# Expert gate and up products: the 96-column chunks share a phase with 128-column ones

## The reference

```
g = jnp.einsum('ech,emh->ecm', buf, Wg)
u = jnp.einsum('ech,emh->ecm', buf, Wu)
out = jnp.einsum('ecm,ehm->ech', jax.nn.silu(g) * u, Wd)
```

## Time and profile before

| | |
|---|---|
| median of 3 runs | 1557.19 us |
| the 3 runs | 1549.15, 1557.19, 1557.39 us |
| span of the profiled execution | 1550.6 us |
| instructions | 30285 |
| TensorE busy | 1471.4 us, 95% of the span |
| VectorE, ScalarE, GpSimd busy | 1132.1, 959.0, 724.0 us |

### The profile page before, as it was taken

The page is one execution under the profiler, slowest core; times in us unless marked ns, Lnnn a source line. Parts: engine busy times, 40 slices in busy tenths (PEclk is TensorE's granted clock), DMA queues, the critical chain, the costliest instruction groups (busy, mean ns, idle before and its releaser), DMA issues.

```text
span 1550.6 us, 30285 instructions
## 1 busy us (share of the span) xinstructions
PE 1471.4 (95%) x10344; PEld 1217.4 (79%) x10344; DVE 1132.1 (73%) x2021; ACT 959.0 (62%) x1897; POOL 724.0 (47%) x894
## 2 busy tenths in 40 slices
PE   6999998999999979599999999999999999999898
PEld 4788887778888767488888888888888888776675
DVE  6677666745888788777777787777777787757666
ACT  4566566644566566677777777777777777731111
POOL 2122225242232155356565655556565655447573
PEclk9999999999999999899999999999999999999999
DMA  6012112332221231398787778777787778567574
GB/s 211 1 63 82 51 60 70 103 93 75 63 76 42 71 108 38 122 370 298 265 296 265 262 259 286 271 268 262 265 297 265 261 261 285 183 213 246 149 216 156
DMA packets 116629, 280.25 MB, mean 181 GB/s; under 512 B 17984, under 2 KB 23104, under 8 KB 116544
## 3 DMA queue, kind: packets, MB, share of 16 engines
q1 hardware_dynamic: 98800, 228.25, 43.4%
q0 software_dynamic: 15360, 50.34, 10.1%
q10 hardware_dynamic: 2384, 0.53, 0.2%
HBM read 235.69 MB, written 43.38 MB: 180 GB/s over the span
## 4 chain that ended last, share of the span: by engine, by line
PE 48%; DVE 3%; issue 2%; POOL 2%; DMA 1%; another core or an unknown queue 1%; ACT 0%; DVEq 0%; SPq 0%; POOLq 0%
PE e_gu L2608 19%; PE e_gu L2610 9%; PE e_dn_rest L2636 6%; PE e_tr L49 3%; PE e_dn_main L41 3%; PE e_dn_main L43 3%; PE e_dn_main L42 3%; DVE h_acc L2901 2%; POOL h_yk L2818 1%; DMA h_yk<-y_dram,h_idx 1%; DVE h_h_raw L2932 0%; DMA e_raw_u<-in_L_ffn_Wu_dram 0%; DVE h_hid L2917 0%; PE h_gt L41 0%
## 5 line engine op out<-in xcount | busy, mean ns | idle before, releaser
L2371 POOL TENSOR_TENSOR e_hid<-e_h_raw,e_hid 128x128 fp32r<-128x128 f32 (+1 forms) x192 | 165.6, 863 | 223.4 <-ACT e_hid L2436 223.4
L2608 PE MATMUL e_gu<-e_xT_hi_lo,e_wg 128*128 128x384 f32 (+1 forms) x768 | 231.9, 358 | 0.6 <-issue 0.6
L2608 PE MATMUL e_gu<-e_xT_hi_lo,e_wu 128*128 128x384 f32 (+1 forms) x768 | 230.6, 356 | 0.0
L2610 PE MATMUL e_gu<-e_xT_hi_lo,e_wu 128*128 128x192 f32 (+1 forms) x768 | 193.4, 252 | 0.0
L2610 PE MATMUL e_gu<-e_xT_hi_lo,e_wg 128*128 128x192 f32 (+1 forms) x768 | 193.2, 252 | 0.0
L2379 POOL TENSOR_TENSOR e_wd<-e_raw_d,e_wd 96x512 fp32r<-96x512 f32 x64 | 131.4, 2053 | 36.1 <-ACT e_wd L2421 36.1
L2431 ACT ACTIVATE e_low<-e_gu 128x384 f32<-128x384 f32 (+1 forms) x192 | 93.2, 486 | 83.5 <-PE e_gu L2610 56.2
L2514 DVE TENSOR_TENSOR e_total<-e_gu,e_low 128x384 f32<-128x384 f32 (+1 forms) x192 | 105.6, 550 | 53.3 <-issue 44.5
L2608 PEld LDWEIGHTS e_gu<-e_xT_hi_lo,e_wg 128*128 128x128 f32 (+1 forms) x768 | 138.3, 180 | 5.8 <-issue 1.6
L2610 PEld LDWEIGHTS e_gu<-e_xT_hi_lo,e_wg 128*128 128x128 f32 (+1 forms) x768 | 140.1, 182 | 1.4
L2608 PEld LDWEIGHTS e_gu<-e_xT_hi_lo,e_wu 128*128 128x128 f32 (+1 forms) x768 | 137.9, 180 | 3.8
(11 more groups left out here) (426 smaller groups left out, 3953.7 us busy)
## 6 DMA issues: line engine op xcount, KB each, us to landing
e_raw_g<-in_L_ffn_Wg_dram SPq DMA_DIRECT2D x64, 704.0 KB
e_raw_u<-in_L_ffn_Wu_dram SPq DMA_DIRECT2D x64, 704.0 KB
e_raw_d<-in_L_ffn_Wd_dram SPq DMA_DIRECT2D x64, 512.0 KB, 6.2
y_dram<-e_y_main SPq DMA_DIRECT2D x64, 256.0 KB
e_raw_d<-in_L_ffn_Wd_dram SPq DMA_DIRECT2D x64, 192.0 KB, 7.5
y_dram<-e_y_rest SPq DMA_DIRECT2D x64, 128.0 KB
s_xr<-in_x_dram SPq DMA_DIRECT2D x16, 256.0 KB, 4.1
x_dram<-s_x SPq DMA_DIRECT2D x16, 256.0 KB, 2.7
```

Source lines behind the costliest of these rows:

```text
L2371: pool.tensor_tensor(hid[b][1][0:n, c, :], h_raw[g.odd][b][0:n, c, 0:P], hid[b][0][0:n, c, :].bitcast(F32), ALU.subtract).then_inc(s_hl, 1)
L2608: pe.matmul(bank[0:n, 0:2 * CAP], w[b][0][:, k, m:m + n], xT[:, :, k, toks], start=k == 0, stop=False)
L2610: ins = pe.matmul(bank[0:n, 0:CAP], w[b][1][:, k, m:m + n], xT[:, 0, k, toks], start=False, stop=k == KC - 1)
```

## The change

The three chunks of an expert's gate and up products become three phases. Phase 0 makes the gate columns of the first chunk (128 wide, into bank half 0) and of the last one (96 wide, half 1). Phase 1 does the same for the up columns. Phase 2 makes gate and up of the middle chunk, both 128 wide. Within a step k the order is now: long product of the second matrix slice, long product of the first, short product of the first, short product of the second. In phases 0 and 1 the second is the 96-column one. The number and the sizes of all products and weight loads stay.

What follows the products changes with it. `total[:, 0]` now holds gates, `total[:, 1]` the matching ups, and `total[:, 2]` gate and up of the middle chunk. Silu, product, rounded copy and low part are two instructions per expert in place of three, one 384 or 256 columns wide over two chunks and one for the middle chunk; they run over all 128 partitions. The product of the first part waits for the sum of phase 1. Hidden slots are in the order first, last, middle, and the down products follow that order. Two memsets of 32 partitions are added on VectorE ahead of the stage's first work there; they write the partitions of a bank half that a 96-column product leaves out.

```
 M = 352
+WIDE, MIDDLE, NARROW = (0, 128), (128, 128), (256, 96)
+HIDDEN = ((0, 128), (2, 96), (1, 128))
+PARTS = (slice(0, 2), slice(2, 3))
+phases = (((wg, WIDE, 0), (wg, NARROW, 1)), ((wu, WIDE, 0), (wu, NARROW, 1)), ((wg, MIDDLE, 0), (wu, MIDDLE, 1)))
...
-for c, (m, n) in enumerate(MCH):
+for c, (one, two) in enumerate(phases):
...
-    for w, bank in ((wg, gu[(b + c) % 2][:, 0]), (wu, gu[(b + c) % 2][:, 1])):
-        for k in range(KC):
-            pe.matmul(bank[0:n, 0:2 * CAP], w[b][0][:, k, m:m + n], xT[:, :, k, toks], start=k == 0, stop=False)
-            ins = pe.matmul(bank[0:n, 0:CAP], w[b][1][:, k, m:m + n], xT[:, 0, k, toks], start=False,
-                            stop=k == KC - 1)
+    for k in range(KC):
+        for w, (m, n), at in (two, one):
+            pe.matmul(gu[(b + c) % 2][0:n, at, 0:2 * CAP], w[b][0][:, k, m:m + n], xT[:, :, k, toks],
+                      start=k == 0, stop=False)
+        for w, (m, n), at in (one, two):
+            ins = pe.matmul(gu[(b + c) % 2][0:n, at, 0:CAP], w[b][1][:, k, m:m + n], xT[:, 0, k, toks],
+                            start=False, stop=k == KC - 1)
     ins.then_inc(s_gu, 1)
...
 # ScalarE, in half
-hidden_hi(g, b, 0)
-silu(g, b, 1)
-low_part(g, b, 2)
-d_hi(g, b, 0)
-hidden_hi(g, b, 1)
-silu(g, b, 2)
-d_hi(g, b, 1)
-hidden_hi(g, b, 2)
+hidden_hi(g, b, 0)
+low_part(g, b, 2)
+d_hi(g, b, 0)
+silu(g, b, 1)
+d_hi(g, b, 1)
+hidden_hi(g, b, 1)
...
 # VectorE, in half (gu_lo 0 and 1 stay where they are)
-sums 0, gu_lo 0, hidden 0, sums 1, gu_lo 1, hidden 1, sums 2, hidden 2, d_lo
+sums 0, gu_lo 0, sums 1, hidden 0, gu_lo 1, sums 2, hidden 1, d_lo
...
+def silu(g, b, i):
+    c = (0, 2)[i]
+    gate = (total[:, 0], total[:, 2, 0:1])[i]
+    act.wait_ge(s_sum, 3 * (2 * g.n + b) + c + 1)
+    act.activation(h_raw[g.odd][b][:, PARTS[i], :], gate, ACT.Silu).then_inc(s_silu, 1)
+def hidden(g, b, i):
+    h = h_raw[g.odd][b][:, PARTS[i], :]
+    up = (total[:, 1], total[:, 2, 1:2])[i]
+    dve.wait_ge(s_silu, 2 * (2 * g.n + b) + i + 1)
+    dve.wait_ge(s_sum, 3 * (2 * g.n + b) + i + 2)
+    dve.tensor_tensor(h, up, h, ALU.mult).then_inc(s_mul, 1)
...
+for m in range(2):
+    dve.memset(gu[m][NARROW[1]:P, 1, :], 0.0)
```

More of the change, by code:

```diff
@@ L2147, in _ @@
             table_part(BATCH, three)
-M, MCH = 352, ((0, 128), (128, 128), (256, 96))
+M = 352
+WIDE, MIDDLE, NARROW = (0, 128), (128, 128), (256, 96)
+HIDDEN = ((0, 128), (2, 96), (1, 128))
+PARTS = (slice(0, 2), slice(2, 3))
 REST = CAP - P
@@ L2363, in hidden_lo @@
             def hidden_lo(g, b):
-                for c, (_, n) in enumerate(MCH):
-                    e = 2 * g.n + b
-                    pool.wait_ge(s_hh, 3 * e + c + 1)
+                for i, part in enumerate(PARTS):
+                    pool.wait_ge(s_hh, 2 * (2 * g.n + b) + i + 1)
                     f = before(g, b, 2)
@@ L2370, in hidden_lo @@
                         pool.wait_ge(s_dm, 2 * f[0].n + b + 1)
-                    pool.tensor_tensor(hid[b][1][0:n, c, :], h_raw[g.odd][b][0:n, c, 0:P],
-                                       hid[b][0][0:n, c, :].bitcast(F32), ALU.subtract).then_inc(s_hl, 1)
-                    if c == 1:
+                    pool.tensor_tensor(hid[b][1][:, part, :], h_raw[g.odd][b][:, part, 0:P],
+                                       hid[b][0][:, part, :].bitcast(F32), ALU.subtract).then_inc(s_hl, 1)
+                    if i == 0:
                         down_lo(g, b)
@@ L2409, in gu_hi @@
                 if f is not None:
-                    act.wait_ge(s_mul, 3 * (2 * f[0].n + b) + 3)
+                    act.wait_ge(s_mul, 2 * (2 * f[0].n + b) + 2)
                 act.activation(w[b][0][:], raw[b][:], ACT.Copy).then_inc(s_guh[b], 1)
@@ L2421, in d_hi, with hidden_hi @@
                 act.activation(wd[b][0][0:rows, cs, :], raw_d[g.odd][b][0:rows, cs, :], ACT.Copy).then_inc(s_dh[b], 1)
-            def silu(g, b, c):
-                n = MCH[c][1]
+            def silu(g, b, i):
+                c = (0, 2)[i]
+                gate = (total[:, 0], total[:, 2, 0:1])[i]
                 act.wait_ge(s_sum, 3 * (2 * g.n + b) + c + 1)
-                act.activation(h_raw[g.odd][b][0:n, c, :], total[0:n, c, 0, :], ACT.Silu).then_inc(s_silu, 1)
+                act.activation(h_raw[g.odd][b][:, PARTS[i], :], gate, ACT.Silu).then_inc(s_silu, 1)
             def low_part(g, b, c):
-                n, m = MCH[c][1], (b + c) % 2
+                m = (b + c) % 2
                 act.wait_ge(s_gu, 3 * (2 * g.n + b) + c + 1)
[L2431 to L2436, removed]
+                act.activation(low[m][:], gu[m][:, :, CAP:2 * CAP], ACT.Copy).then_inc(s_low, 1)
+            def hidden_hi(g, b, i):
+                act.wait_ge(s_mul, 2 * (2 * g.n + b) + i + 1)
+                act.activation(hid[b][0][:, PARTS[i], :], h_raw[g.odd][b][:, PARTS[i], 0:P], ACT.Copy).then_inc(s_hh, 1)
             def x_hi(g, b):
@@ L2510, in sums @@
             def sums(g, b, c):
-                n, m = MCH[c][1], (b + c) % 2
+                m = (b + c) % 2
                 dve.wait_ge(s_low, 3 * (2 * g.n + b) + c + 1)
[L2514 to L2520, removed]
+                dve.tensor_tensor(total[:, c], gu[m][:, :, 0:CAP], low[m][:], ALU.add).then_inc(s_sum, 1)
+            def hidden(g, b, i):
[4 more added lines that the diff above has]
+                dve.tensor_tensor(h, up, h, ALU.mult).then_inc(s_mul, 1)
             def x_lo(g, b):
@@ L2548, in half @@
                     ahead.split_lo(dve, 0, 2)
+                sums(g, b, 1)
                 hidden(g, b, 0)
-                sums(g, b, 1)
                 if more:
@@ L2554, in half @@
                     ahead.split_lo(dve, 2, 4)
+                sums(g, b, 2)
                 hidden(g, b, 1)
-                sums(g, b, 2)
-                hidden(g, b, 2)
                 d_lo(g, b)
+            for m in range(2):
+                dve.memset(gu[m][NARROW[1]:P, 1, :], 0.0)
             dve.wait_ge(s_nT, 1)
@@ L2600, in gate_up @@
                 toks = slice(b * CAP, (b + 1) * CAP)
-                for c, (m, n) in enumerate(MCH):
+                for c, (one, two) in enumerate(phases):
                     if not (isinstance(g.n, int) and 3 * e + c < 2):
                         pe.wait_ge(s_sum, 3 * e + c - 1)
-                    for w, bank in ((wg, gu[(b + c) % 2][:, 0]), (wu, gu[(b + c) % 2][:, 1])):
-                        for k in range(KC):
-                            pe.matmul(bank[0:n, 0:2 * CAP], w[b][0][:, k, m:m + n], xT[:, :, k, toks], start=k == 0,
-                                      stop=False)
-                            ins = pe.matmul(bank[0:n, 0:CAP], w[b][1][:, k, m:m + n], xT[:, 0, k, toks], start=False,
-                                            stop=k == KC - 1)
+                    for k in range(KC):
[5 more added lines that the diff above has]
+                                            start=False, stop=k == KC - 1)
                     ins.then_inc(s_gu, 1)
@@ L2618, in down_main @@
                 pe.wait_ge(s_dp[b], g.n + 1)
-                pe.wait_ge(s_hl, 3 * e + 3)
+                pe.wait_ge(s_hl, 2 * e + 2)
                 if before(g, b, 1) is not None:
                     pe.wait_ge(s_ym, e)
-                for c, (_, n) in enumerate(MCH):
-                    ins = matmul3(pe, dn_main[:], (hid[b][0][0:n, c, :], hid[b][1][0:n, c, :]),
-                                  (wd[b][0][0:n, c, :], wd[b][1][0:n, c, :]), c == 0, c == 2)
+                for i, (c, n) in enumerate(HIDDEN):
+                    ins = matmul3(pe, dn_main[:], (hid[b][0][0:n, i, :], hid[b][1][0:n, i, :]),
+                                  (wd[b][0][0:n, c, :], wd[b][1][0:n, c, :]), i == 0, i == 2)
                 ins.then_inc(s_dm, 1)
             def down_rest(g):
-                pe.wait_ge(s_mul, 3 * (2 * g.n + 2))
+                pe.wait_ge(s_mul, 2 * (2 * g.n + 2))
                 for b in range(2):
@@ L2633, in down_rest @@
                     pe.wait_ge(s_yr, g.n)
-                for c, (_, n) in enumerate(MCH):
+                for i, (c, n) in enumerate(HIDDEN):
                     for b in range(2):
-                        ins = pe.matmul(dn_rest[b * REST:(b + 1) * REST, :], h_raw[g.odd][b][0:n, c, P:CAP],
-                                        raw_d[g.odd][b][0:n, c, :], start=c == 0, stop=c == 2)
+                        ins = pe.matmul(dn_rest[b * REST:(b + 1) * REST, :], h_raw[g.odd][b][0:n, i, P:CAP],
+                                        raw_d[g.odd][b][0:n, c, :], start=i == 0, stop=i == 2)
                 ins.then_inc(s_dr, 1)
```

## The result

The changed kernel takes 1543.46 us, the median of 4 runs (1540.01 to 1547.57), and the kernel before, run beside it, 1555.85 (1549.15 to 1557.39). The ratio is 0.994, with a 95% interval of 0.9921 to 0.996. A later set of runs gave 1543.18 against 1552.75 us, 0.9928 (0.9901 to 0.9955). The change is faster, by 0.4 to 1%, near the forecast of 1546.6 us; the medians differ by 12.4 and by 9.6 us, where 10.55 were forecast. The profiled execution has a span of 1538.3 us, where the one before had 1550.6.

A forecast was written before the change was run, and what follows sets the result against it. TensorE's own instructions were taken to bound the expert stage. Loads took 10.75 us off and the start added 0.2: a span of 1540.05 us, or 1557.19 - 10.55 = 1546.6 us as median; range 1537 to 1558.5.

The forecast's parts named there:

- exposed loads: 128-column weight loads behind short products on TensorE: 15 per expert before, 8 after; 7 x 24 ns x 64 = 10.75 us off.
- the range: Measured time expected between 1537 and 1558.5 us.
- Banks: Each step of phases 0 and 1 changes banks twice, 24 changes per expert against 6; cost taken as 0.
- the rival: Changes of bank cost 10 ns each on TensorE, eating the gain: 1558.1 us; chance 0.08.
- VectorE's and GpSimd's cover: 0.67 us to spare ahead of gate_up, 0.55 ahead of phase 2, 3.2 covering GpSimd's first low part; cost 0.
- The wide product's price: VectorE's 384-wide first product, shown in no row, taken as 0.55 us.
- The start: Two memsets ahead of VectorE's first casts, at most 1.4 us, delay the stage by 0 to 0.8; 0.2 us taken.
- The merged instructions: Fewer, wider Silus, products, copies and low parts save VectorE 0.42 us and ScalarE 0.23 per expert; worth 0 in time.
- the sum: Span forecast: 1550.6 - 10.75 + 0.2 = 1540.05 us.

The follow-up runs named there:

- the repeat: The changed kernel run again without any edit, against the kernel before: ratio 0.9928 (0.9901 to 0.9955), a turn of 21.467 us.

## Why the prediction was right

**The step that carried it** was the count and price of exposed loads: 7 per expert, 24 ns each, 10.75 us. The turn fell by 0.333 us, the forecast was 0.34; 32 such turns are 10.7 us. The two kernels that undo the order alone lose 0.62 us a turn (ratio 1.0054) and all but 0.04 us of the gain. The place was right as well: behind a long product a 128-column load costs nothing, and a turn with 64 columns is only 0.03 us shorter than one with 96.

**The price of one load** is not one number. It was 23.8 ns from before to after, 20.7 and 20.9 in the two runs that changed the order, and 22.6 in the one that changed the width. The forecast took 24 from whole pairs and would have been 1.3 us too high with 21; the range held that.

**Part of the close agreement is luck.** For each expert alone the forecast of 0.168 us was off, by a fifth for the one behind the transposes (0.135) and by a quarter for the other (0.213), and 0.014 us came back elsewhere in the turn. Per load these are 19 and 30 ns. The misses nearly cancel. What they consist of is mostly the step of phases 0 and 1, 533 and 525 ns for the two experts, where the forecast had 530 for both.

**Banks** cost nothing that shows: no run tries them alone, but each step of phases 0 and 1 has two changes and takes 525 to 534 ns, where two pairs of 96 columns took 2 x 265 = 530. At most 4 ns a step could be theirs, not the 20 that the rival needed.

**VectorE's and GpSimd's cover** held: 0.69 us was to spare ahead of gate_up (0.67 worked out) and 0.54 us ahead of phase 2 (0.55). The wide product's price, 0.56 us, came from the nearest shape, the 384-wide sum.

**The start** shows 0.07 us and not 0.2, but two executions of the changed kernel differ by as much; the memsets took 0.5 us each.

**What the sum left out** is the end. The merged instructions were put at nothing, which holds in the turns. Behind the last gate_up, though, the chain before ran over GpSimd: its low part of the down weights (2.17 us), then a stretched low part (1.59), then the down product.

```profile
...
1354.05 2.17 POOL e_wd L2379
1356.22 1.59 POOL e_hid L2371
```

After the change GpSimd's two last operations there are these:

```profile
...
1344.72 2.06 POOL L2385 TENSOR_TENSOR e_wd<-e_raw_d,e_wd 96x512 fp32r<-96x512 f32 x1 [1.04 <-ACT e_wd L2427]
1346.75 0.45 POOL L2377 TENSOR_TENSOR e_hid<-e_h_raw,e_hid 128x128 fp32r<-128x128 f32 x1
```

The low part takes 0.45 us at 1346.75, and the chain runs over the next transposes instead. But that is this execution's: in the repeat the chain runs over GpSimd as before, with 2.07 us (at 1347.81) and a low part of 0.98. From the last full turn to the final `down_rest` it is 18.48 us before, and 16.83 and 1353.44 - 1336.08 = 17.36 after, of which one gate_up's gain explains 0.14. So 1.0 to 1.5 us came at the end, with one trace of the kernel before to compare with. That the merged instructions bring it is not shown.

**The time itself**: the sum against the profiled execution was 1540.05 us of span, and 1538.3 came out. The difference of 1.8 us is the end's 1.5 us, the shared stage's 1.7 and, the other way, the 1.5 us by which the stage begins later. The last two are within what executions of one kernel differ by.

## What to carry to other kernels

Where TensorE is at 100%, read the distance from start to start for each kind of product, and look at which weight load stands behind which product. Here a 128-column load stuck out behind a 192-column product, by some 20 to 24 ns, and cost nothing behind a 384-column one; 96 columns were all but hidden behind either. So put wide loads behind long products and narrow ones behind short ones, and count the positions before and after: count times price was right to 1% of a turn's gain here, and to about a quarter for each expert alone. Don't break up a row of products that may overlap each other, and take the price of a block boundary from that boundary's own rows.

## What the runs showed of the hardware that I had not expected

- The load that just hides behind a 192-column product has about 96 columns: over a turn, 64 gain 0.9 ns each, 112 cost 8.0 and 128 cost 22.6.
- Products in full fp32 with 64 columns of weights take 0.455 us each in a row, where they run two by two, and 1.00 us apart, between products of the other kind.
- A long product takes 257 to 263 ns to the next start where it is the first behind the transposes, with a load of 64, 96 or 128 columns, and 173 to 180 behind a 512-column product.
- The same step of four products takes 525 ns for the expert that starts behind a 512-column product (916.35 to 918.45 for four) and 534 for the one behind the transposes, through both phases (907.77 to 911.51 for seven). With 64-column loads the latter's gate_up fell from 6.65 to 6.60 us, and the former's rose from 6.50 to 6.52 (means of the turns from 730 to 1330 us, from its first start to the next operation's). With the middle phase first, where the narrow steps of both experts follow exposed loads, both have 533. It looks as if a row of loads that fit exactly never catches up once it is late; no run here takes this apart.
